# ScalarE takes the first norm's root of unit n + 1 ahead of its copy of the turned rows of unit n

## The chip, the cores and the metric

One Trainium2 chip, of which one core runs the kernel. The metric is the time of one execution on the device, in microseconds, as the median of several runs. The engines are TensorE (PE; its weight loads are PEld), VectorE (DVE), ScalarE (ACT), GpSimd (POOL) and SyncE (SP), which issues most of the transfers. Each engine runs its own program in order, and they meet by semaphores.

## The reference, cut to what matters

A block of a small vision model, on x of shape (2, 256, 32, 32) in fp32: a norm over the channels, an attention with 1x1 convolutions, and a mixture of eight experts on the tokens.

```python
def _ln_c(v, eps=1e-06):
    m = jnp.mean(v, axis=1, keepdims=True)
    s = jnp.var(v, axis=1, keepdims=True)
    return (v - m) / jnp.sqrt(s + eps)
...
# in _L0_conv_ref, with xf = _ln_c(x) as (b, c, n)
g_vec = jnp.mean(jax.nn.softmax(xf, axis=2) * xf, axis=2)
g_map = jnp.broadcast_to(g_vec[:, :, None], (b, c, n))
kv_in = jnp.concatenate([g_map, xf], axis=1)
q = _proj(_proj(xf, q_w1, q_g1, q_b1), q_w2, q_g2, q_b2)
k = _proj(_proj(kv_in, k_w1, k_g1, k_b1), k_w2, k_g2, k_b2)
v = _proj(kv_in, v_w, v_g, v_b)
sim = jnp.einsum('bcn,bcm->bnm', q, k) * tc ** (-0.5)
attn = jax.nn.softmax(sim, axis=-1)
ctx = jnp.einsum('bnm,bcm->bcn', attn, v)
out = _proj(ctx, o_w, o_g, o_b)
...
x = x + _L0_conv_ref(_ln_c(x), ...)
t = _to_tokens(x)
t = t + _L0_ffn_ref(_ln_t(t), ...)   # top 2 of 8 experts, 256 -> 1024 -> 256, gelu
x = _from_tokens(t, x)
```

The change lies in the first line of work, `_ln_c(x)`: the norm of each of the 2048 positions over its 256 channels.

## The kernel before, in words

The 2048 rows (positions) are cut into 4 units of 512, and a unit into 4 blocks of 128 rows. For each unit the first norm goes through five engines:

- SyncE loads the unit's rows into `x1` (L359), one transfer of 512 KB each, the four of them issued first, with the query weights between.
- VectorE, `row_stats(u)`: four `bn_stats` (L854) and four `bn_aggr` (L858) give mean and variance, `mv1`; each aggregate raises `var_ready`.
- ScalarE, `root(u)` (L598): one small activation takes the square root of the four variances into `rstd1`, and raises `std_ready`.
- VectorE, `row_norm(u)`: waits for that, takes the reciprocal in place (L864, raises `rstd_ready`), and norms blocks 0 and 1 of the unit into `xn2` (L867, `normed`). GpSimd waits for `rstd_ready` and norms blocks 2 and 3 (L450, `normed_more`).
- TensorE, `turn_rows(u)` (L1254): eight transposes of 128x128 against the identity, two a block, into two PSUM banks; the last raises `xn_turned`. Units 0 and 2 share banks, and so do units 1 and 3, so the transposes of unit u also wait for the copy of unit u - 2.
- ScalarE, `channels(u)` (L604): one copy of 128x1024 from PSUM into `x_cn`, the rows in channel order; it raises `xcn_ready`.

VectorE's program has, unit after unit, `row_stats(u)` and `row_norm(u)`, so the statistics of the next unit stand behind the norms of this one. TensorE's program is: transposes of units 0 and 1; first query projection of unit 0 (`project("q1", 0)`, L1271, needs `xcn_ready` of unit 0); transposes of unit 2; q1 of unit 1; second query projection q2 of unit 0 (L1266); transposes of unit 3; q2 of unit 1; then the query projections of units 2 and 3, then the key and value projections. ScalarE takes each projection out of PSUM (`take`, L622), and its program mixes these with the copies; behind the take of q2 of unit 1 come a table load and the exponentials of the softmax over positions for batch 0 (L636), which need the maximum that VectorE takes over units 0 and 1 (L872). Two more takes of q1 follow.

Behind all this stand the key and value projections, 16 steps of attention with the output convolution, the second norm and routing, and from about 170 us on the experts, which fill the rest of the time. The order on each engine is written out by hand; no scheduler decides it. TensorE begins the kernel with nine matmuls on ones (L1240).

Of the kernel before, what the change touches and what calls it, by code (L numbers as in the profile page):

```python
# [52 lines left out]
def metaformer_kernel(nc, x_tok_d, q1_d, q2_d, k1_d, k2_d, v_d, o_d, aff_d, og_d, ob_d,  # L53
                      wg_d, w1_d, b1_d, w2_d, b2_d, out_d):
    ctx = ExitStack()
    with ctx:
# [351 lines left out]
        def _(pool):  # L408
# [162 lines left out]
            for e in range(E):  # L571
                _, t1, odd, more = expert_bounds(pool, e)

                odd1 = pool.value_load(bounds[0:1, 1, e:e + 1], min_val=0, max_val=E)
                with pool.If(odd):
                    tile(t0, e, t0 * 2 + odd0, WIDE)
                with pool.Else():
                    tile(t0, e, t0 * 2 + odd0, 2)
                with pool.If(more):
                    with pool.Fori(t0 + 1, t1) as t:  # L580
                        tile(t, e, t * 2 + odd1, 2)
                t0 = t1
                odd0 = odd1
# [6 lines left out]
        def _(act):  # L590
# [5 lines left out]
            def root(u):  # L596
                act.wait_ge(var_ready, BLKU * (u + 1))
                act.activation(rstd1[:, u * BLKU:(u + 1) * BLKU], mv1[:, u * BLKU:(u + 1) * BLKU, 1], ACT.Sqrt,  # L598
                               bias=eps_c[:, :]).then_inc(std_ready, 1)

            def channels(u):

                act.wait_ge(xn_turned, u + 1)
                act.activation(x_cn[:, :, u * UNIT:(u + 1) * UNIT], banks[:, TURN_BANK[u]:TURN_BANK[u] + 2, :],  # L604
                               ACT.Copy).then_inc(xcn_ready, 1)
# [25 lines left out]
            def global_exp(b):  # L631
                act.wait_ge(gmax_ready, b + 1)
                for k in range(KC):
                    if b:
# [2 lines left out]
                                   ACT.Exp, bias=gmax[:, b, k:k + 1], accum_out=gsum[:, b, k:k + 1]  # L637
                                   ).then_inc(gexp_ready, 1)

            for u in range(2):  # L640
                root(u)
                channels(u)
            root(2)
            root(3)
            act.wait_ge(wq_loaded, 16 * 3)
            take("q1", 0)
# [9 lines left out]
            for b in range(B):  # L656
                u, w = 2 * b, 2 * b + 1
# [170 lines left out]
        def _(dve):  # L828
# [388 lines left out]
            for e in range(E):  # L1217
                _, t1, odd, more = experts[e]
                with dve.If(odd):
                    tile(t0, e, WIDE, True)  # L1220
                with dve.Else():
                    tile(t0, e, 2, True)
                with dve.If(more):
                    with dve.Fori(t0 + 1, t1) as t:
                        tile(t, e, 2, False)
                t0 = t1
# [379 lines left out]
```

## Time and profile before

| what | value |
|---|---|
| median of 3 runs | 427.2 us (425.88 to 430.45) |
| profiled execution | 429.23 us, of which the span of its core is 427.5 |
| mean granted TensorE clock | 0.918 of full speed |
| TensorE busy, matmuls | 372.4 us, 87% of the span |
| TensorE busy, weight loads | 333.8 us, 78% |
| VectorE busy | 264.9 us, 62% |
| ScalarE busy | 247.6 us, 58% |
| GpSimd busy | 177.3 us, 41% |
| chain that ended last | TensorE 38%, GpSimd 10%, issue 8% |

The span runs from the first to the last instruction; the rest of an execution's time lies around it. The granted clock is the share of TensorE's full speed that the chip allowed: 1.00 is 2.4 GHz and 0.50 is 1.2 GHz. In a timeline, a row is a run of like instructions, with its start, its length from the first one's start to the last one's end, their count, and in brackets how long the engine stood idle ahead of them and what released it. Rows of one engine can overlap by a tenth of a microsecond, since an instruction begins before the one ahead of it has drained.

### The profile page before, as it was taken

How to read it: one execution, taken by the hardware profiler on the slowest of the kernel's cores; microseconds unless marked ns; L12 is line 12 of the kernel's file. 1: busy time of each engine (PE TensorE's matmuls, PEld its weight loads, DVE VectorE, ACT ScalarE, POOL GpSimd, SP SyncE). 2: the span in 40 equal slices, each digit the busy share in tenths (PEclk: the TensorE clock that was granted, in tenths of full speed). 3: DMA queues.
4: the chain of work that ended last, by engine and by line, in shares of the span. 5: the costliest groups of instructions: out<-in, count | busy, mean ns of one | idle time of the engine just before them, and what ended most of it. 6: DMA issues, size and time to landing. Idle time of an engine off the chain costs nothing.

```text
span 427.5 us, 8138 instructions
## 1 busy us (share of the span) xinstructions
PE 372.4 (87%) x2476; PEld 333.8 (78%) x2477; DVE 264.9 (62%) x693; ACT 247.6 (58%) x522; POOL 177.3 (41%) x271
## 2 busy tenths in 40 slices
PE   5789969997998866999969999989999999989960
PEld 4435557886787856999969998989989999989960
DVE  5668487797889896364438444874448754834430
ACT  1386656656525872575539555795557955764530
POOL 5620000003045444326642665656546546656553
PEclk9699999999996555799998999999999999999995
DMA  8710000000010764609322832378323724232333
GB/s 277 231 37 2 0 1 2 0 2 1 2 61 39 299 204 133 236 15 255 57 53 27 246 62 54 49 237 244 60 56 46 240 40 71 39 53 53 49 52 35
DMA packets 22966, 38.63 MB, mean 90 GB/s; under 512 B 2576, under 2 KB 17296, under 8 KB 22800
## 3 DMA queue, kind: packets, MB, share of 16 engines
q0 software_dynamic: 8032, 12.82, 17.9%
q1 hardware_dynamic: 14896, 25.41, 17.2%
q8 instruction: 11, 0.18, 0.2%
q14 instruction: 27, 0.22, 0.2%
HBM read 28.85 MB, written 9.37 MB: 89 GB/s over the span
## 4 chain that ended last, share of the span: by engine, by line
PE 38%; POOL 10%; issue 8%; DVE 2%; POOLq 1%; DMA 1%; DVEq 1%; ACT 1%; ACTq 0%
POOL xg L521 8%; PE banks L1534 6%; PE banks L1233 6%; PE banks L1234 6%; PE banks L1235 6%; PE banks L1536 5%; PE banks L1538 5%; PE banks L1511 3%; DVE h_lo L1183 1%; DVE y_out L1207 1%; PE banks L1566 1%; POOL idx_in L516 1%; DMA xg<-xn_rows,idx_in 1%; POOL idx_out L559 1%; POOL out_rows L567 0%
## 5 line engine op out<-in xcount | busy, mean ns | idle before, releaser
L790 ACT ACTIVATE h_raw<-banks,b1t 128x256 f32<-128x256 f32 (+1 forms) x136 | 67.6, 497 | 86.7 <-PE banks L1235 86.1
L1183 DVE TENSOR_TENSOR h_lo<-h_raw,h_hi 128x256 fp32r<-128x256 f32 (+1 forms) x136 | 58.0, 441 | 65.0 <-ACT h_hi L793 63.0
L1534 PE MATMUL banks<-w_hi,h_hi 128*128 128x256 f32 x288 | 84.3, 293 | 9.2 <-DVE h_lo L1183 9.2
L1234 PE MATMUL banks<-x_lo,w_hi 128*128 128x256 f32 (+1 forms) x272 | 79.3, 292 | 3.5 <-issue 3.5
L1536 PE MATMUL banks<-w_lo,h_hi 128*128 128x256 f32 x288 | 81.4, 283 | 0.0
L1538 PE MATMUL banks<-w_hi,h_lo 128*128 128x256 f32 x288 | 81.4, 283 | 0.0
L1233 PE MATMUL banks<-x_hi,w_hi 128*128 128x256 f32 (+1 forms) x272 | 80.2, 295 | 0.8 <-issue 0.8
L1235 PE MATMUL banks<-x_hi,w_lo 128*128 128x256 f32 (+1 forms) x272 | 79.4, 292 | 0.0
L567 POOL DMA_INDIRECT out_rows<-y_out,idx_out x36 | 62.5, 1736 | 33.7 <-DVE y_out L1207 27.9
L521 POOL DMA_INDIRECT xg<-xn_rows,idx_in x57 | 57.1, 1001 | 27.9 <-POOL idx_in L516 16.3
L793 ACT ACTIVATE h_hi<-banks,b1t 128x256 fp32r<-128x256 f32 (+1 forms) x136 | 67.4, 495 | 0.0
L1534 PEld LDWEIGHTS banks<-w_hi,h_hi 128*128 128x128 f32 x288 | 55.2, 192 | 11.9 <-DVE h_lo L1183 11.8
L1235 PEld LDWEIGHTS banks<-x_hi,w_lo 128*128 128x128 f32 x272 | 52.7, 194 | 3.6 <-issue 3.6
L1536 PEld LDWEIGHTS banks<-w_lo,h_hi 128*128 128x128 f32 x288 | 55.2, 192 | 0.0
L1538 PEld LDWEIGHTS banks<-w_hi,h_lo 128*128 128x128 f32 x288 | 55.1, 191 | 0.0
L1233 PEld LDWEIGHTS banks<-x_hi,w_hi 128*128 128x128 f32 x272 | 52.8, 194 | 1.9 <-issue 1.8
L1234 PEld LDWEIGHTS banks<-x_lo,w_hi 128*128 128x128 f32 x272 | 52.8, 194 | 0.0
L472 POOL TENSOR_TENSOR rt<-rstd_i,rhv 128x4 f32<-128x4 f32 x12 | 2.5, 211 | 97.9 <-DVE rstd_i L990 97.2
L1190 DVE TENSOR_TENSOR w_lo<-w_raw,w_hi 128x512 fp32r<-128x512 f32 x56 | 38.5, 688 | 1.0
L803 ACT ACTIVATE w_hi<-w_raw 128x512 fp32r<-128x512 f32 x56 | 36.8, 656 | 0.0
L680 ACT ACTIVATE pt_hi<-banks 128x512 fp32r<-128x512 f32 x32 | 17.5, 596 | 20.9 <-PE banks L1348 20.9
L1207 DVE TENSOR_SCALAR y_out<-y_sum,score 128x256 f32<-128x256 f32 x36 | 11.0, 350 | 23.1 <-POOLq L562 22.8
(219 smaller groups left out, 681.0 us busy)
## 6 DMA issues: line engine op xcount, KB each, us to landing
w_raw<-in_w SPq DMA_DIRECT2D x16, 1024.0 KB, 8.2
xn_rows<-xn SPq DMA_DIRECT2D x2, 1056.0 KB, 5.0
x<-in_x_tok SPq DMA_DIRECT2D x4, 512.0 KB, 4.9
out_rows<-x SPq DMA_DIRECT2D x1, 2048.0 KB, 9.3
b2b<-in_b SPq DMA_DIRECT2D x1, 1024.0 KB, 4.8
xg<-xn_rows,idx_in POOLq DMA_INDIRECT x57
out_rows<-y_out,idx_out POOLq DMA_INDIRECT x36, 4.0
out_rows<-x POOLq DMA_DIRECT2D x1, 384.0 KB, 3.2
```

The source lines that it names most:

```text
L521: pool.indirect_dma_start(xg[:, i, :], None, xs_d, bass.IndirectOffsetOnAxis(ap=idx_in[:, i:i + 1], axis=0)).then_inc(x_gathered, 16)
L567: pool.indirect_dma_start(out_d, bass.IndirectOffsetOnAxis(ap=idx_out[:, i:i + 1], axis=0), y_out[:, i, :], None, compute_op=ALU.add).then ...
L790: act.activation(h_raw[j % RING][:, 0:w], banks[:, j % RING, 0:w], ACT.Gelu, bias=bias)
L793: act.activation(h_hi[:, j, 0:w], banks[:, j % RING, 0:w], ACT.Gelu, bias=bias).then_inc(gelu_done, 1)
L1183: dve.tensor_tensor(h_lo[:, j, 0:w], h_raw[j % RING][:, 0:w], h_hi[:, j, 0:w].bitcast(F32), ALU.subtract).then_inc(h_split, 1)
L1190: dve.tensor_tensor(w_lo[(e + 1) % 2][:, c], w_raw[(e + 1) % 2][:, c], w_hi[(e + 1) % 2][:, c].bitcast(F32), ALU.subtract).then_inc(w_spli ...
L1233: pe.matmul(out, a_hi, b_hi, start=start, stop=False)
L1234: pe.matmul(out, a_hi, b_lo, start=False, stop=False)
L1235: return pe.matmul(out, a_lo, b_hi, start=False, stop=stop)
L1534: pe.matmul(out, h_hi[:, j, r], w_hi[e % 2][:, c], start=j == 0 and i < 2, stop=False, skip_group_check=width == WIDE)
L1536: pe.matmul(out, h_hi[:, j, r], w_lo[e % 2][:, c], start=False, stop=False, skip_group_check=width == WIDE)
L1538: ins = pe.matmul(out, h_lo[:, j, r], w_hi[e % 2][:, c], start=False, stop=j == HJ - 1, skip_group_check=width == WIDE)
```

## The change

In ScalarE's program the roots of units 1 and 2 are taken one place earlier: that of unit n + 1 now stands ahead of the copy of unit n. The root of unit 3 keeps its place. No instruction is added or removed, and no other engine's program is touched.

```diff
--- before.py
+++ after.py
@@ -637,10 +637,10 @@
                                    ACT.Exp, bias=gmax[:, b, k:k + 1], accum_out=gsum[:, b, k:k + 1]
                                    ).then_inc(gexp_ready, 1)
 
+            root(0)
             for u in range(2):
-                root(u)
+                root(u + 1)
                 channels(u)
-            root(2)
             root(3)
             act.wait_ge(wq_loaded, 16 * 3)
             take("q1", 0)
```

ScalarE at the start of its program, before: the rows on `rstd` are the roots, the rows on `x_cn` the copies, the rows on `q1r` and `q2r` the takes, and the brackets name the semaphores waited for.

```order
L593 ACT_TABLE_LOAD
L593 ACTIVATE warm<-eps_c 128x1 [waits consts_made]
L598 ACTIVATE rstd<-mv,eps_c 128x4 [waits var_ready]
L604 ACTIVATE x_cn<-banks 128x2x512 [waits xn_turned]
L598 ACTIVATE rstd<-mv,eps_c 128x4 [waits var_ready]
L604 ACTIVATE x_cn<-banks 128x2x512 [waits xn_turned]
L598 ACTIVATE rstd<-mv,eps_c 128x4 [waits var_ready] x2
L622 ACTIVATE q1r<-banks,aff 128x512 [waits proj_ready,wq_loaded]
```

The roots of units 2 and 3 stood together behind the second copy. The same place of ScalarE's program with the change:

```order
L593 ACT_TABLE_LOAD
L593 ACTIVATE warm<-eps_c 128x1 [waits consts_made]
L598 ACTIVATE rstd<-mv,eps_c 128x4 [waits var_ready] x2
L604 ACTIVATE x_cn<-banks 128x2x512 [waits xn_turned]
L598 ACTIVATE rstd<-mv,eps_c 128x4 [waits var_ready]
L604 ACTIVATE x_cn<-banks 128x2x512 [waits xn_turned]
L598 ACTIVATE rstd<-mv,eps_c 128x4 [waits var_ready]
L622 ACTIVATE q1r<-banks,aff 128x512 [waits proj_ready,wq_loaded]
```

Now two roots stand ahead of the first copy and one ahead of the second; the table loads are where they were. The other end of the relay is TensorE, whose program is the same in both kernels; this is its piece from the first query projection of unit 0 over the transposes of unit 2 to the projection of unit 1.

```order
L1271 MATMUL banks<-x_cn,w_q 128x512 [waits xcn_ready,wq_loaded]
L1271 MATMUL banks<-x_cn,w_q 128x512
L1254 MATMUL banks<-ident,xn 128x128 [waits normed,xcn_ready]
L1254 MATMUL banks<-ident,xn 128x128
L1254 MATMUL banks<-ident,xn 128x128 [waits normed]
L1254 MATMUL banks<-ident,xn 128x128
L1254 MATMUL banks<-ident,xn 128x128 [waits normed_more]
```

Nothing moved here: the transposes of unit 2 stand behind the projection, and wait in turn for VectorE's norms, for the copy of unit 0 and for GpSimd's norms.

## Rows read from the trace of the kernel before

**Rows 1.** Timeline of ScalarE, 4 to 30 us: start us, us, engine, line, tiles.
```profile
10.57 1.02 ACT L604 ACTIVATE x_cn<-banks 128x1024 f32<-128x1024 f32 x1 [3.67 <-PE banks L1254]
11.49 0.29 ACT L598 ACTIVATE rstd<-mv,eps_c 128x4 f32<-128x4 f32 x1
15.43 1.02 ACT L604 ACTIVATE x_cn<-banks 128x1024 f32<-128x1024 f32 x1 [3.65 <-PE banks L1254]
16.35 0.29 ACT L598 ACTIVATE rstd<-mv,eps_c 128x4 f32<-128x4 f32 x1
19.41 0.30 ACT L598 ACTIVATE rstd<-mv,eps_c 128x4 f32<-128x4 f32 x1 [2.77 <-DVE mv L858]
19.61 0.76 ACT L622 ACTIVATE q1r<-banks,aff 128x512 f32<-128x512 f32 x1
...
23.50 1.02 ACT L604 ACTIVATE x_cn<-banks 128x1024 f32<-128x1024 f32 x1
...
25.21 1.28 ACT L636 ACT_TABLE_LOAD   x1
...
28.78 1.43 ACT L622 ACTIVATE q1r<-banks,aff 128x512 f32<-128x512 f32 x2
```

**Rows 2.** Timeline of VectorE, 4 to 22 us.
```profile
9.28 0.35 DVE L858 BATCH_NORM_AGGREGATE mv<-bst 128x2 f32<-128x6 f32 x4
11.81 0.18 DVE L864 RECIPROCAL rstd<-rstd 128x4 f32<-128x4 f32 x1 [2.18 <-ACT rstd L598]
...
12.85 1.39 DVE L854 BATCH_NORM_STATS2 bst<-x 128x6 f32<-128x256 f32 x4
14.16 0.35 DVE L858 BATCH_NORM_AGGREGATE mv<-bst 128x2 f32<-128x6 f32 x4
...
19.02 0.35 DVE L858 BATCH_NORM_AGGREGATE mv<-bst 128x2 f32<-128x6 f32 x4
```

**Rows 3.** Timeline of GpSimd, 4 to 30 us.
```profile
7.22 2.57 POOL L450 TENSOR_SCALAR xn<-x,mv,rstd 128x256 f32<-128x256 f32 x2 [3.39 <-DVE rstd L864]
12.09 2.56 POOL L450 TENSOR_SCALAR xn<-x,mv,rstd 128x256 f32<-128x256 f32 x2 [2.30 <-DVE rstd L864]
16.95 2.56 POOL L450 TENSOR_SCALAR xn<-x,mv,rstd 128x256 f32<-128x256 f32 x2 [2.30 <-DVE rstd L864]
```

**Rows 4.** Timeline of TensorE's matmuls, 4 to 25 us.
```profile
9.85 0.69 PE L1254 MATMUL banks<-ident,xn 128*128 128x128 f32 x2 [0.64 <-POOL xn L450]
12.50 1.70 PE L1254 MATMUL banks<-ident,xn 128*128 128x128 f32 x6 [1.96 <-DVE xn L867]
14.71 0.69 PE L1254 MATMUL banks<-ident,xn 128*128 128x128 f32 x2 [0.51 <-POOL xn L450]
15.19 3.62 PE L1271 MATMUL banks<-x_cn,w_q 128*128 128x512 f32 x4
18.60 1.41 PE L1254 MATMUL banks<-ident,xn 128*128 128x128 f32 x8
19.85 1.88 PE L1271 MATMUL banks<-x_cn,w_q 128*128 128x512 f32 x4
...
22.42 1.04 PE L1254 MATMUL banks<-ident,xn 128*128 128x128 f32 x8
```

**Rows 5.** The line that issues the four loads of x, and their landing.
```profile
L359 SPq DMA_DIRECT2D x<-in_x_tok x4: 382/426/467, 0.8 to 2.7; - x4
...
DMA to landing us min/median/max: 3.4/4.9/6.3
```

**Rows 6.** Windows of TensorE: stretch, its length, busy us (count), granted clock, DMA.
```profile
8.90:19.10 10.20, 7.08 (x19) 0.50 0.98 295
19.00:19.20 0.20, 0.20 (x4) 0.88 0.07 26
128.50:131.60 3.10, 3.10 (x16) 0.50 0.22 90
171.80:175.90 4.10, 4.10 (x20) 0.50 0.94 356
```

## The prediction

> **What bounds the kernel now.** I read the page first, and in it the busy shares: TensorE is busy 87% of the span, VectorE and ScalarE about 60%. The page's chain of the work that ended last is shown from 167 us on only, so the front is read from the timelines of the four engines, each for its own waits, and then from the windows, for the granted clock. The edit touches nothing behind ScalarE's copy for unit 1, so the first 30 us are what has to be understood.
>
> The front is a relay by units of 512 rows. VectorE makes the statistics, ScalarE the root, VectorE the reciprocal and two norms, GpSimd the other two norms, TensorE turns the four blocks, ScalarE copies the result to channel order. [rows 1] show ScalarE's place in it. It finishes the copy for unit 0 at 11.59 and only then takes the root of unit 1, at 11.49 by the overlapped records. That root's input was ready long before: VectorE's last aggregate for unit 1 starts at 9.28 and ends at 9.63 [rows 2]. The engine stood idle for 3.67 us before the copy, waiting for TensorE. VectorE then waits 2.18 us for the root. The same happens for unit 2: the statistics end at 14.51 [rows 2], the copy for unit 1 runs at 15.43, the root at 16.35. VectorE can't run ahead, since its program is in order and the reciprocal stands ahead of the next unit's statistics.
>
> GpSimd is the slowest hand: its two norms of a unit take 2.56 us [rows 3], and TensorE's last two transposes of unit 1 start at 14.71, just behind GpSimd's end at 14.65. TensorE does the first projection next, 15.19 to 18.60, then unit 2's transposes, and from there it waits little: two projections, unit 3's transposes, and so on, each row beginning as the one before it ends [rows 4]. ScalarE's copy of unit 3 (23.50) follows the transposes that end at 23.46, its next take follows at once, and the table load for the exponentials comes at 25.21. Behind it the exponentials and the two takes at 28.78 run back to back, while TensorE stands still. So **from unit 1's transposes to 28.78 there is one path: TensorE up to 23.5, ScalarE from there**, and what shortens the front moves all that follows.
>
> **The change, part by part.** Nothing is added or removed: still four roots of 0.29 us and four copies of 1.02 us. Three roots move. No table load appears between them, as the printed order shows.
>
> *Root of unit 1.* It is ready when the aggregates end, 9.63. In unit 3, where ScalarE stands waiting at the root, it starts 0.04 after them (19.37 to 19.41, [rows 1, 2]). So it starts at 9.67 in place of 11.49: **1.82 us earlier**. The reciprocal comes 0.32 behind the root (11.49 to 11.81) at 9.99; GpSimd 0.28 behind that, at 10.27, in place of 12.09. GpSimd is free since 9.79 (its unit 0) and TensorE since 10.54, so neither takes anything back. Unit 1's transposes end 1.82 earlier, at 13.58, and the copy for unit 1 starts at 13.61, not 15.43. The copy for unit 0 keeps its 10.57, since the root ahead of it ends at 9.97.
>
> *Root of unit 2.* VectorE's statistics start at 12.85 - 1.82 = 11.03 and end 1.66 later (12.85 to 14.51), at 12.69. Unit 2's rows must be there by 11.03 and unit 3's by 14.1: the last of the four loads is issued at 2.7 and the longest takes 6.3 us to land, so 9.0 at the latest [rows 5]. The root takes 12.73 to 13.02, in place of 16.35: 3.62 earlier. What queues behind it on ScalarE is the copy for unit 1, wanted at 13.58: **0.56 us of cover**. GpSimd does unit 2 at 13.33 to 15.89, not 16.95 to 19.51.
>
> *Root of unit 3.* Its order against the copy for unit 1 is as before. Statistics start at 14.08, end at 15.75 (the same 1.66); the root at 15.79 meets a free ScalarE. GpSimd ends unit 3 at 16.39 + 2.56 = 18.95, and its reader on TensorE comes behind 20, so the rest of this gain is worth nothing. VectorE's maximum for batch 0 comes earlier too; its reader, the exponential, stands behind ScalarE's takes and gains nothing by that.
>
> *TensorE.* The first projection starts at 15.19 - 1.82 = 13.37 and occupies 3.41 us (15.19 to 18.60), to 16.78. Now unit 2's norms have been ready since 15.89, so its transposes wait for nothing. At the full clock eight occupy 0.88 us (22.42 to 23.30). At the low clock two occupy 0.48 (14.71 to 15.19), or 0.44 taken as twice the fast time; I take 1.76 for eight. In the trace the granted clock is at its lower level, 1.2 GHz, from 8.9 on and returns to 2.4 GHz at 19.05 (its mean of 0.88 over 19.0 to 19.2 leaves 0.05 us at 0.50, [rows 6]), 3.86 after the projection began. If it comes back as long after the same work, at 17.23, then 0.45 of the slow 1.76 is spent, and the other 74% take 0.66: the transposes end at 16.78 + 0.45 + 0.66 = 17.89. Before it was 19.85: **1.96 us earlier**, of which 0.14 is a wait for GpSimd that is gone.
>
> ScalarE's take of the first projection then starts at about 17.0; it was held until 19.61 by the root of unit 3, but its reader on TensorE comes one projection at the full clock later (half of 3.41), at 17.89 + 1.71 = 19.60, and finds it done. All behind keeps its lengths: 1.96 earlier at 23.5, at 25.21 and at 28.78. The key and value weights were issued by about 9 and the projections that want them stand behind 28 us, so no load holds them.
>
> **The sum.** 1.96 us off an execution of 429.23 (span 427.5, 1.7 around it) is 427.3. The median of the runs shown is 427.2, 2.0 below the profiled one, so I subtract from the median: 425.2.
>
> **A rule against the row.** The row: the clock is low from 8.9 to 19.05, and returns inside a stretch in which TensorE has been busy without a gap since 14.71 [rows 4, 6]. My sum lets it return by the work. The Trainium skill, page "TensorE: Matmul & The Clock Gate", section "What's actually happening", says the chip's looking at activity is free-running and isn't reset by the kernel's start, so the switch falls differently from run to run. By this rule the sum may keep 19.05 as the moment, or take an earlier one. One trace can't tell which; it gives rivals 1 and 2 their chances.
>
> **The rivals.**
> 1. *The clock returns at the same moment of the trace, 19.05.* Transposes all slow: 16.78 + 1.76 = 18.54. The next projection is slow for 0.51 and loses half of it, 0.25. Gain 19.85 - 18.54 - 0.25 = 1.06. Time 426.1. For it: nothing that moves the clock's own times is in the edit. Against: busy work starts earlier too. Chance 0.17.
> 2. *The clock returns sooner*, since TensorE's pause between units 0 and 1 (10.54 to 12.50) is gone. The bound is GpSimd's end of unit 2 at 15.89: last pair of transposes 15.95 to 16.17, gain 19.85 - 16.17 = 3.68. Half way between this and 1.96 is 2.8. Time 424.4, at the far end 423.5. For it: denser work from 10.68 on. Against: in the trace the clock stayed low through the transposes of unit 1 too. Chance 0.20.
> 3. *The other side: the later low stretches grow.* All that follows 28.78 runs 2 us earlier, and the clock need not follow. One spell of low clock lasted 3.1 us with TensorE always busy; the end of the long one, 171.8 to 175.9, is 4.1 us of pure TensorE at half speed [rows 6]. Each lengthened by such a spell costs half of it, 1.6 to 2.0. The place is the first transposes and products of the expert stage. Beyond 4 us more of low clock under pure TensorE the gain is eaten; slower by 1% needs (4.3 + 2.0) x 2 = 12.6 us. I take 8 us: time 429.2. For it: the runs of before differ by 4.6 us with no edit at all. Against: the spells can as well get shorter. Chance 0.08.
> 4. *It doesn't do what it says.* If unit 2's rows landed after 11.6 (11.03 and the 0.56 of cover), the root ahead would hold the copy of unit 1, and past 13.4 it would be later than before: 427.2 and up. [rows 5] put the landing 2.6 us short of the first point. Chance 0.05.
>
> **How the numbers follow.** The forecast has 0.50: 425.2. A measurement of this kernel tells about 1% from no change, 4.3 us, so faster means under 422.9 and slower over 431.5. The runs of before lie from 425.88 to 430.45, 1.3 below and 3.3 above their median; a median is surer, and I give it 1.5 to either side. Under 422.9 lie a third of rival 2 (0.07), whose far end is 0.6 above it, and a tenth of the forecast (0.05): 0.12. Over 431.5 lies half of rival 3, 0.04. The rest is 0.84. The range reaches from rival 2's far end less some of the spread to short of rival 3's time: 421.9 to 428.5.
>
> **What would show it.** In the new timeline the root of unit 1 at 9.67, ahead of the copy at 10.57; GpSimd's norms at 10.3, 13.3 and 16.4; no idle of VectorE over 0.4 us ahead of a reciprocal; the copy for unit 1 at 13.6; unit 2's transposes beginning at 16.8 and ending near 17.9; the table load at 23.2; the two takes behind the exponentials at 26.8. The windows give the clock's return near 17.2 (forecast), 19.0 (rival 1) or before 16 (rival 2). The prediction fails if the table load moves by less than 1 us or more than 3, or if it moves by 2 and the span doesn't: then the gain is lost to the clock or to a wait behind 30 us.

## The result and the profile after

The changed kernel takes 424.96 us as the median of 10 executions (424.21 to 427.16). The kernel before, run beside it and now over 10 executions, takes 428.35 (425.88 to 430.45). The ratio is 0.9925, with a 95% interval of 0.9904 to 0.9947: 3.2 us faster, by between 2.3 and 4.1. (The ratio is not the quotient of the two medians, which differ by 3.4.) The forecast was 425.2 and "within 1%", and both hold. But the median it was taken from, 427.2 over three executions, was 1.2 us below what ten gave, and the forecast step of 1.96 us lies below the interval of the measured one.

| | before | after |
|---|---|---|
| profiled execution | 429.23 us | 427.16 us |
| its span | 427.5 us | 425.4 us |
| TensorE busy, matmuls | 372.4 us | 372.0 us |
| ScalarE busy | 247.6 us | 248.1 us |
| VectorE busy | 264.9 us | 264.9 us |
| GpSimd busy | 177.3 us | 177.6 us |

The work is the same to half a microsecond; what went is waiting. ScalarE in the changed kernel, timeline from 4 us on (start, length, engine, line, tiles, in brackets the idle time ahead and who ended it), which answers to [rows 1]:

```profile
9.68 0.30 ACT L598 ACTIVATE rstd<-mv,eps_c 128x4 f32<-128x4 f32 x1 [2.77 <-DVE mv L858]
10.59 1.02 ACT L604 ACTIVATE x_cn<-banks 128x1024 f32<-128x1024 f32 x1 [0.61 <-PE banks L1254]
12.75 0.30 ACT L598 ACTIVATE rstd<-mv,eps_c 128x4 f32<-128x4 f32 x1 [1.14 <-DVE mv L858]
13.63 1.02 ACT L604 ACTIVATE x_cn<-banks 128x1024 f32<-128x1024 f32 x1 [0.59 <-PE banks L1254]
15.82 0.30 ACT L598 ACTIVATE rstd<-mv,eps_c 128x4 f32<-128x4 f32 x1 [1.16 <-DVE mv L858]
...
23.07 1.28 ACT L636 ACT_TABLE_LOAD   x1
...
26.65 1.43 ACT L622 ACTIVATE q1r<-banks,aff 128x512 f32<-128x512 f32 x2
```

The root of unit 1 stands at 9.68 and not at 11.49, that of unit 2 at 12.75 and not at 16.35. Both roots now start when VectorE's aggregates are done (`DVE mv`), within 0.04 us, and the copies behind them still wait for TensorE, 0.61 and 0.59 us. The second of these is the cover that was worked out as 0.56: the time by which the root ends before the copy's input is there. The table load at 23.07 was at 25.21, and the two takes at 26.65 were at 28.78: 2.14 and 2.13 us. Two reciprocals of VectorE, after, against the one at 11.81 in [rows 2] that had waited 2.18 us:

```profile
10.01 0.18 DVE L864 RECIPROCAL rstd<-rstd 128x4 f32<-128x4 f32 x1 [0.36 <-ACT rstd L598]
...
13.08 0.18 DVE L864 RECIPROCAL rstd<-rstd 128x4 f32<-128x4 f32 x1 [0.36 <-ACT rstd L598]
```

GpSimd's norms of units 1 to 3, which answer to [rows 3] (units 1 and 2 at 12.09 and 16.95 there):

```profile
10.29 2.56 POOL L450 TENSOR_SCALAR xn<-x,mv,rstd 128x256 f32<-128x256 f32 x2 [0.48 <-DVE rstd L864]
13.36 2.56 POOL L450 TENSOR_SCALAR xn<-x,mv,rstd 128x256 f32<-128x256 f32 x2 [0.50 <-DVE rstd L864]
16.42 2.56 POOL L450 TENSOR_SCALAR xn<-x,mv,rstd 128x256 f32<-128x256 f32 x2 [0.50 <-DVE rstd L864]
```

TensorE's matmuls from the last transposes of unit 1 on, against [rows 4]:

```profile
12.91 0.69 PE L1254 MATMUL banks<-ident,xn 128*128 128x128 f32 x2 [0.52 <-POOL xn L450]
13.39 3.61 PE L1271 MATMUL banks<-x_cn,w_q 128*128 128x512 f32 x4
16.80 1.07 PE L1254 MATMUL banks<-ident,xn 128*128 128x128 f32 x8
17.71 1.88 PE L1271 MATMUL banks<-x_cn,w_q 128*128 128x512 f32 x4
19.43 1.02 PE L1266 MATMUL banks<-q1r,w_q 128*128 128x512 f32 x2
```

Turning unit 1 ends at 13.60, the first projection runs 13.39 to 16.80, and the transposes of unit 2, which had waited in part for GpSimd, take 0.91 us (16.80 to 17.71) and not 1.25. The next projection starts at 17.71 in place of 19.85. This is the whole of the gain in this pair of executions: 2.14 us at the second projection (the one of unit 1), 2.14 at the table load, 2.1 in the span.

One row misleads. The window of TensorE over the first projection (stretch, its length, busy us, granted clock, DMA) says:

```profile
13.40:16.60 3.20, 3.20 (x5) 1.00 0.98 351
```

A clock of 1.00, and yet four matmuls of 512 columns occupy 3.41 us, exactly as in the trace of before, where [rows 6] give 0.50. Four such matmuls at the full clock occupy 1.72 (17.71 to 19.43 in the timeline above). So this projection ran at 1.2 GHz although its window says 2.4. The windows of this trace show nothing below 1.00 ahead of 126 us. The trace of before has the same blind start: its opening matmuls take 421 ns or more each and the shortest transposes of unit 0 take 272 ns, all under a window of 1.00, and the first low clock in its windows is the fall at 8.8. In the changed kernel's trace the transposes of unit 0 take 421 ns or more, so its clock was low already. The eight transposes at 16.80 take 0.91 us, close to the 0.88 of the full clock, so the clock came back at about 16.8; this is read from lengths, not from the record.

### The profile page after: what moved, and what is told of

Its sections match the earlier page's. It is cut to its first block, busy times and chain, and to the rows that moved or that the text cites. A ratio compares the mean times of both kernels' runs of the same rounds, so it can differ in the third digit from the quotient of the medians.

```text
span 425.4 us, 8138 instructions
## 1 busy us (share of the span) xinstructions
PE 372.0 (87%) x2476; PEld 333.7 (78%) x2477; DVE 264.9 (62%) x693; ACT 248.1 (58%) x522; POOL 177.6 (42%) x271
## 4 chain that ended last, share of the span: by engine, by line
PE 38%; POOL 10%; issue 8%; DVE 2%; DMA 1%; POOLq 1%; DVEq 1%; ACT 1%; ACTq 0%
POOL xg L521 8%; PE banks L1534 6%; PE banks L1233 6%; PE banks L1234 6%; PE banks L1235 6%; PE banks L1536 5%; PE banks L1538 5%; PE banks L1511 3%; DVE h_lo L1183 1%; DVE y_out L1207 1%; PE banks L1566 1%; DMA xg<-xn_rows,idx_in 1%; POOL idx_in L516 1%; POOL idx_out L559 1%; POOL out_rows L567 0%
## 5 line engine op out<-in xcount | busy, mean ns | idle before, releaser
L680 ACT ACTIVATE pt_hi<-banks 128x512 fp32r<-128x512 f32 x32 | 17.5, 596 | 20.9 <-PE banks L1348 20.9
```

## The experiments

Twelve runs followed. The theory: there is one path through the front (all work ahead of the table load), each unit's blocks come late by what ScalarE's root is late, the front gives between 1 and 3.7 us as the clock returns late or early, and all behind it keeps its length. The rivals: both moves carry the gain alike; the clock and not the order is what costs; a second gain lies behind the front. The table gives each kernel's time against the kernel before in the same comparison (ratio, its interval, and the ratio's distance from 1 in us). Its last column says where the table load stands in the profiled execution, which measures the front alone.

| kernel | ratio (95%) | us against before | table load |
|---|---|---|---|
| before, second profile | 0.9993 (0.9969 to 1.0016) | -0.3 | 25.23 |
| changed, first | 0.9925 (0.9904 to 0.9947) | -3.2 | 23.07 |
| changed, second | 0.9924 (0.9894 to 0.9953) | -3.2 | 22.39 |
| changed, third | 0.9919 (0.9888 to 0.9951) | -3.5 | 23.35 |
| root of unit 1 alone | 0.9971 (0.9949 to 0.9993) | -1.2 | 23.39 |
| root of unit 2 alone | 1.0006 (0.9986 to 1.0025) | +0.3 | 25.62 |
| all roots first | 1.0072 (1.0042 to 1.0102) | +3.1 | 28.11 |
| before, extra matmuls | 0.9946 (0.9918 to 0.9975) | -2.3 | 24.74 |
| changed, extra matmuls | 0.9897 (0.9856 to 0.9938) | -4.4 | 21.61 |
| changed, 1 memset late | 0.9962 (0.9937 to 0.9988) | -1.6 | 23.92 |
| changed, 2 memsets late | 0.9953 (0.9927 to 0.9979) | -2.0 | 24.84 |
| changed, three norms on VectorE | 0.9935 (0.9910 to 0.9960) | -2.8 | 21.61 |
| the same, extra matmuls | 0.9912 (0.9882 to 0.9943) | -3.8 | 21.62 |

**The changed kernel again, twice.** No edit.

> The changed kernel once more, beside the runs of the two parts. Theory (one path through the front, shortened at unit 1): the table load for the exponentials stands near 23.1 us in place of 25.2, and the time is 2.1 us under the kernel before. Rival (there is a second gain somewhere behind 30 us): the time is 3 us or more under it while the table load moves by only 2.1.

> The changed kernel a third time. Theory (the front gives 2.1 to 2.8 us by the moment of the clock's return, the rest is the same on average): the table load between 22.3 and 23.6, and a ratio that, with the two measured so far, tends to 2.1 to 2.8 us under the kernel before. Rival (a second gain of about 1 us behind the front): again 3.2 us or more.

The step holds: -3.2 and -3.5 us, not the 2.1 to 2.8 that the theory expected. The rival of both, a second gain behind the front, was marked by 3 us or more and by 3.2 or more, and both times met it; the first mark also asked for a table load that moves by 2.1 alone, and there it moved by 2.8. The front isn't a constant, though. TensorE in the second profile of the changed kernel:

```profile
13.38 2.93 PE L1271 MATMUL banks<-x_cn,w_q 128*128 128x512 f32 x4
16.15 1.04 PE L1254 MATMUL banks<-ident,xn 128*128 128x128 f32 x8
17.02 1.88 PE L1271 MATMUL banks<-x_cn,w_q 128*128 128x512 f32 x4
```

Two windows of TensorE in the same trace, with the granted clock as the number behind the count:

```profile
15.30:15.50 0.20, 0.20 (x1) 0.53 0.91 348
15.50:15.70 0.20, 0.20 (x1) 1.00 1.01 410
```

The clock came back at 15.5, inside the first projection, which then occupied 2.77 us and not 3.41; the transposes began at 16.15, held by nothing, since GpSimd ends unit 2 at 15.9. The table load stands at 22.39, 2.82 us ahead of before: rival 2 of the prediction, with its own number. The third profile has its transposes from 16.80 to 17.99 and the table load at 23.35, 1.86 ahead; from their 1.19 us, against 0.88 fast and 1.76 slow, the clock came back at about 17.4. So the front gives 1.9 to 2.8 us, 2.3 as the mean of three.

**The kernel before again.** No edit.

> The kernel before against itself, as a measure of what the comparison can tell, and one more profile of it. Theory: the table load at 24.9 to 25.7 us, whatever the moment at which the clock comes back in the front, since GpSimd's norms of unit 2 end at 19.5; what differs between two executions lies behind 30 us, in where the stretches of low clock fall, and the span from the table load to the end is anything from 400 to 402.5. The ratio within 0.3% of 1. Rival (the front decides the spread of the runs): the table load differs by over 1 us from 25.2.

The front and the ratio are as expected. The rest is not: from the table load to the end this profile takes 405.2 us, where 400 to 402.5 was expected and the first profile has 402.3. TensorE in this second profile of before:

```profile
15.21 2.89 PE L1271 MATMUL banks<-x_cn,w_q 128*128 128x512 f32 x4
17.94 0.89 PE L1254 MATMUL banks<-ident,xn 128*128 128x128 f32 x6
19.59 0.44 PE L1254 MATMUL banks<-ident,xn 128*128 128x128 f32 x2 [0.77 <-POOL xn L450]
19.87 1.88 PE L1271 MATMUL banks<-x_cn,w_q 128*128 128x512 f32 x4
```

Here, too, the clock returned early: the projection occupies 2.73 us, not 3.41, and the transposes begin at 17.94 in place of 18.60. It buys nothing: the last two wait 0.77 us for GpSimd, the second projection starts at 19.87 and the table load stands at 25.23, within 0.02 of the first profile. In the kernel before, an early clock is lost at GpSimd; in the changed one it is kept. That is why the change is worth more than 1.96 at the table load in an execution with an early clock.

**The two halves of the change.**

```diff
 root of unit 1 alone
 root(0)
-channels(0)
 root(1)
+channels(0)
 channels(1)
 root(2)
 root(3)
```

```diff
 root of unit 2 alone
 root(0)
 channels(0)
 root(1)
-channels(1)
 root(2)
+channels(1)
 root(3)
```

> Only the root of unit 1 goes ahead of the copy of unit 0; the root of unit 2 stays behind the copy of unit 1. Theory: unit 1's transposes end 1.8 us earlier, unit 2's norms on GpSimd end at 17.7 instead of 15.9, which delays the transposes of unit 2 by 0.1 us at most if the clock is low until about 17, so the table load stands at 23.2 and the time is within 0.5 us of the whole change. Where the clock comes back sooner, GpSimd's 17.7 binds and up to 1.5 us of the gain are missing. Rival (both moves carry the gain alike): the table load at 24 or later, the time 1 us above the whole change.

> Only the root of unit 2 goes ahead of the copy of unit 1; the root of unit 1 stays behind the copy of unit 0. Theory: unit 1's transposes stay at 15.4, the first projection at 15.2, and the only gain is that GpSimd ends unit 2 at 17.7 and not at 19.5; unit 2's transposes begin at 18.6 as before and end at most 0.2 us earlier with the clock as in the kernel before, up to 1.2 with an earlier clock. Time 0 to 1 us under the kernel before. Rival (both moves carry it): 1 to 1.6 us.

The profile of each half follows. The root of unit 1 alone, TensorE:

```profile
13.38 3.42 PE L1272 MATMUL banks<-x_cn,w_q 128*128 128x512 f32 x4
16.63 0.82 PE L1255 MATMUL banks<-ident,xn 128*128 128x128 f32 x6
17.76 0.44 PE L1255 MATMUL banks<-ident,xn 128*128 128x128 f32 x2 [0.31 <-POOL xn L450]
18.03 1.88 PE L1272 MATMUL banks<-x_cn,w_q 128*128 128x512 f32 x4
```

The projection starts at 13.38, as in the full change. The last transposes of unit 2 then wait 0.31 us for GpSimd (worked out: ready at 17.7, here 17.76) and the second projection starts at 18.03. With the root of unit 2 moved as well that bound is at 15.9. So in the front the first move carries 1.8 us, and the second adds what an early clock allows: 0.0 to 1.0 in the three profiles of the full change, 0.5 on average. The time doesn't agree. Root of unit 1 alone takes 1.2 us off (0.3 to 2.2), where within 0.5 of the whole change was expected, and beside it in the same comparison the whole change took 3.2 off, a median of 424.24 against 426.02. So the rival's mark in the time, 1 us above the whole change, is met, and its mark at the table load, 24 or later, is not (23.39). Of those 2 us the front accounts for 0.5; the rest isn't explained.

The root of unit 2 alone, TensorE:

```profile
15.20 3.62 PE L1272 MATMUL banks<-x_cn,w_q 128*128 128x512 f32 x4
18.61 1.81 PE L1255 MATMUL banks<-ident,xn 128*128 128x128 f32 x8
20.26 1.88 PE L1272 MATMUL banks<-x_cn,w_q 128*128 128x512 f32 x4
```

And GpSimd's norms of units 1 and 2 in the same trace:

```profile
12.10 2.56 POOL L450 TENSOR_SCALAR xn<-x,mv,rstd 128x256 f32<-128x256 f32 x2 [2.30 <-DVE rstd L865]
15.17 2.56 POOL L450 TENSOR_SCALAR xn<-x,mv,rstd 128x256 f32<-128x256 f32 x2 [0.51 <-DVE rstd L865]
```

GpSimd has unit 2 ready 1.8 us earlier (15.17 and not 16.95), TensorE doesn't use it, as its first projection still starts at 15.20. In this execution the clock was late and the transposes took 1.65 us; the time is that of the kernel before within its interval (0.6 us less to 1.1 more). That the second move alone is worth its rival's 1 to 1.6 us is out, and in the front the two don't carry the gain alike. The two times, -1.2 and +0.3, do not add up to the -3.2 of both. Some of that is as the theory has it, since the second move pays only behind the first; the size is not.

**All roots first.**

```diff
 root(0)
 root(1)
-channels(0)
 root(2)
-channels(1)
 root(3)
+channels(0)
+channels(1)
```

> All four roots stand ahead of the first copy. Theory: the root of unit 3 is ready at 15.75, so the copy of unit 0 starts at 16.1 and not at 10.6, the first projection at about 17.2 and not at 13.4 (it waits for that copy); the table load stands at 27 to 28 us, and the time is 1.5 to 3 us above the kernel before. Rival (an earlier root is always better since the copy has cover): no later than the changed kernel.

+3.1 us, the table load at 28.11, each a tenth beyond what was expected. ScalarE's root of unit 3, its two copies and the table load:

```profile
15.81 0.30 ACT L598 ACTIVATE rstd<-mv,eps_c 128x4 f32<-128x4 f32 x1 [2.77 <-DVE mv L859]
16.01 1.92 ACT L604 ACTIVATE x_cn<-banks 128x1024 f32<-128x1024 f32 x2
...
28.11 1.28 ACT L636 ACT_TABLE_LOAD   x1
```

TensorE's first projection in the same trace:

```profile
17.16 3.75 PE L1272 MATMUL banks<-x_cn,w_q 128*128 128x512 f32 x4 [3.57 <-ACT x_cn L604]
```

The copy of unit 0 went from 10.59 to 16.01, since the root of unit 3 waits for its statistics until 15.8. The projection waits 3.57 us for it, and starts at 17.16, as worked out. An earlier root is no good in itself: it may stand ahead of a copy as long as it ends before the copy's input comes.

**Extra matmuls, to have the clock back early.** They go into a bank that is written anew before anything is read from it, and compute nothing that is used.

```diff
-            for _ in range(9):
+            for _ in range(15):
                 pe.matmul(banks[:, 7, 0:P], ones[:, :], ones[:, :], start=True, stop=True)
...
                 for j in range(BLKU):
+                    if u < 2:
+                        for _ in range((1, 1, 1, 2)[j] if u == 0 else (4, 1, 1, 2)[j]):
+                            pe.matmul(banks[:, 3, 0:P], ones[:, :], ones[:, :], start=True, stop=True)
```

> The kernel before with extra matmuls on ones: 15 in place of 9 at the start, and a few in TensorE's waits among the transposes of units 0 and 1, into a bank that nobody reads. They compute nothing that is used. Theory: the clock is back before the first projection (15.2), which then takes 1.7 us; but the transposes of unit 2 wait for GpSimd, whose norms of unit 2 end at 19.5, so they end at 19.8 as before and the table load stays at 25.2. Time within 0.5 us of the kernel before. Rival (the low clock in the front is what costs): 1.5 us or more under it.

> The changed kernel with the same extra matmuls. Theory: GpSimd's norms of unit 2 end at 15.9, the first projection at full clock ends at 15.1, so the transposes of unit 2 end at 16.2 and the table load stands at 21.5 us: 3.7 us ahead of the kernel before, and 0.9 to 1.6 us ahead of the changed kernel's profiles (22.4 and 23.1). Time 3.5 to 4.5 us under the kernel before. Rival (GpSimd or ScalarE binds earlier than worked out): the table load at 22.4 or later, and no difference from the changed kernel.

In the kernel before with them, ScalarE:

```profile
10.34 1.02 ACT L604 ACTIVATE x_cn<-banks 128x1024 f32<-128x1024 f32 x1 [3.43 <-PE banks L1257]
11.26 0.29 ACT L598 ACTIVATE rstd<-mv,eps_c 128x4 f32<-128x4 f32 x1
...
24.74 1.28 ACT L636 ACT_TABLE_LOAD   x1
```

TensorE in the same trace:

```profile
14.76 1.88 PE L1274 MATMUL banks<-x_cn,w_q 128*128 128x512 f32 x4
16.98 1.36 PE L1257 MATMUL banks<-ident,xn 128*128 128x128 f32 x6 [0.34 <-DVE xn L867]
19.10 0.44 PE L1257 MATMUL banks<-ident,xn 128*128 128x128 f32 x2 [0.77 <-POOL xn L450]
```

The projection runs at the full clock, 14.76 on, the transposes begin at 16.98, and the last two stand 0.77 us until GpSimd is done: the clock alone is lost there, as the theory has it. What I had missed is the 0.47 us ahead of that. At the full clock the transposes of unit 0 end sooner, the copy starts at 10.34 and not 10.57, and the root behind it at 11.26 and not 11.49; twice 0.23 makes the table load's 24.74. The time fell by 2.3 us, by at least 1.1, where I expected under 0.5; the rival, that the low clock in the front is what costs, was marked by 1.5 or more. The front accounts for 0.5 of it; the rest isn't explained, so by the time this rival is not out. In the changed kernel with them, TensorE:

```profile
13.18 1.88 PE L1274 MATMUL banks<-x_cn,w_q 128*128 128x512 f32 x4
14.90 0.82 PE L1257 MATMUL banks<-ident,xn 128*128 128x128 f32 x6
15.98 0.44 PE L1257 MATMUL banks<-ident,xn 128*128 128x128 f32 x2 [0.26 <-POOL xn L450]
16.25 1.88 PE L1274 MATMUL banks<-x_cn,w_q 128*128 128x512 f32 x4
```

The second projection starts at 16.25 (worked out: 16.2) and the table load stands at 21.61, 3.6 us ahead of before. Both are met, and so is the time, 4.4 us under before, the lowest of all kernels here, though its interval (2.7 to 6.2) overlaps that of the change.

**The relay late by a known amount.** One or two idle memsets of 128x1024 on VectorE ahead of the first statistics, on the changed kernel.

```diff
+            for i in range(2):      # or range(1)
+                dve.memset(prob[i][:, :], 0.0)
             for u in range(UNITS):
                 row_stats(u)
```

> The changed kernel with one idle memset of 128x1024 on VectorE ahead of the first statistics, about 1.1 us, which shifts the whole relay and nothing else. Theory (one path, and all behind it keeps its length): the time is 1.1 us above the changed kernel, 2.1 under the kernel before. Rival (the measured gain of 3.2 holds a part that comes from how the rest of the kernel lies against the chip's clock, and not from the front): the time moves by something else than 1.1, such as 0 or 2.

> The same with two memsets, about 2.1 us. Theory: 2.1 us above the changed kernel, 1.1 under the kernel before. Rival: the front shift that the profiled pair shows (2.1) is given back whole, and the time is that of the kernel before, or it differs from the step of late1 by much more or less than 1.1.

The memsets delay the root of unit 1 by 1.0 and 2.1 us (10.69 and 11.76 against 9.68). Measured are -1.6 and -2.0 us against before. From the change's -3.3 (mean of three) that is 1.7 and 1.3 later, where the table loads moved by 1.0 and 1.9 from the mean of 22.9. The first is met within its uncertainty of about 1.1 us. The second is 0.8 short of its mark of 2.1, and one memset and two can't be told apart by time: the step between them, expected as 1.1 more, is 0.4 less. With two memsets the kernel still takes at least 0.9 us less than before, with a table load only 0.4 ahead. The memsets suggest that a late front costs time; a slope of 1 they don't show.

**Three of four norms on VectorE**, with and without the extra matmuls.

```diff
-        DVE_NORMS = 2
+        DVE_NORMS = 3
```

> The changed kernel with three of a unit's four norms on VectorE and one on GpSimd. Theory (after the change a unit's blocks are late by GpSimd's two norms of 2.56 us): unit 1's last norm is ready at about 12.0 and not 12.85, the first projection starts at about 12.5 and not 13.4, and the table load comes 0.9 us earlier than in the changed kernel, at 21.5 to 22.2; the time 0.9 us under the changed kernel. Rival (VectorE, whose turn per unit grows from 3.07 to 3.48 us, is late instead): no gain or a loss.

> The same with the extra matmuls on ones. Theory: the clock is back before the first projection at 12.4, which ends at 14.1; unit 2's last norm is ready at about 15.5, so its transposes end at 15.8, and the table load stands at 21.1 us, 0.5 ahead of the kernel with the extra matmuls and two norms each, 4.1 ahead of the kernel before. Time 4 to 5 us under the kernel before. Rival: VectorE's longer turn makes unit 2 and 3 late and the table load stays at 21.6.

TensorE without the extra matmuls:

```profile
12.84 2.58 PE L1271 MATMUL banks<-x_cn,w_q 128*128 128x512 f32 x4
15.26 1.04 PE L1254 MATMUL banks<-ident,xn 128*128 128x128 f32 x8
```

ScalarE in the same trace:

```profile
16.79 0.30 ACT L598 ACTIVATE rstd<-mv,eps_c 128x4 f32<-128x4 f32 x1 [2.18 <-DVE mv L858]
17.00 0.76 ACT L622 ACTIVATE q1r<-banks,aff 128x512 f32<-128x512 f32 x1
...
20.79 0.80 ACT L622 ACTIVATE q2r<-banks,aff 128x512 f32<-128x512 f32 x1
21.61 1.28 ACT L636 ACT_TABLE_LOAD   x1
```

The first projection starts 0.55 us earlier than in the changed kernel, at 12.84 and not at 12.5 as worked out: unit 1's norms are ready at 12.0, but its eight transposes begin at 11.03 and occupy 1.81 us in a row at the low clock, so TensorE itself is last. GpSimd, 1.40 us a unit, binds no more. But the table load stands at 21.61 and 21.62 without and with the extra matmuls, the same as with two norms and the extra matmuls (21.61). From the root of unit 3 at 16.79 to the table load ScalarE has no idle time at all: take, copy, take, take, copy, take. What starts this row is VectorE: that root waits 2.18 us for the statistics (`DVE mv`), since VectorE's turn per unit is 3.39 us here (root to root, 13.40 to 16.79) and not 3.07. So the rival of the second run, a table load that stays at 21.6 by VectorE's longer turn, is what came, with ScalarE's row behind it. The first projection ends at 15.26, and its take stands behind this root until 17.00: a small case of what all roots first shows; no run here tries this take ahead of the root. The times, -2.8 and -3.8 us, are not below the change's beyond the intervals; the first was expected at 0.9 under the change, and is 0.5 above it.

**Where the rest of the difference is.** Cut at the table load, at the start of the last exponential of the attention, at the first and the last transpose of the expert stage, the traces give in us:

| kernel | to table load | attention | routing | experts | end |
|---|---|---|---|---|---|
| before | 25.2 | 88.2 | 56.9 | 239.7 | 17.5 |
| before, second | 25.2 | 89.6 | 57.5 | 240.6 | 17.5 |
| changed | 23.1 | 88.2 | 57.4 | 239.2 | 17.5 |
| changed, second | 22.4 | 89.1 | 57.0 | 236.6 | 17.5 |
| changed, third | 23.4 | 88.2 | 57.1 | 238.1 | 17.6 |
| root of unit 1 alone | 23.4 | 89.1 | 57.0 | 236.8 | 17.5 |
| root of unit 2 alone | 25.6 | 89.6 | 57.0 | 236.3 | 17.5 |
| all roots first | 28.1 | 89.6 | 56.8 | 237.8 | 17.6 |
| before, extra matmuls | 24.7 | 89.6 | 57.0 | 237.9 | 17.5 |
| changed, extra matmuls | 21.6 | 88.2 | 57.0 | 234.9 | 17.5 |
| 1 memset late | 23.9 | 88.2 | 57.2 | 237.0 | 17.5 |
| 2 memsets late | 24.8 | 88.2 | 57.2 | 236.8 | 17.5 |
| three norms | 21.6 | 89.1 | 57.4 | 237.9 | 17.6 |
| three norms, extra | 21.6 | 89.1 | 57.4 | 234.1 | 17.6 |

No column behind the first follows the edits one for one. The expert stage runs the same program in all and takes anything from 234.1 to 240.6 us; two profiles of one and the same kernel differ by up to 2.6 us there. That is large beside the 3 to 6 us over which the executions of one kernel spread. The two profiles of before are the longest of all there (239.7 and 240.6), and the two with the change and the extra matmuls are the shortest (234.9 and 234.1). The traces hold one thing that goes with it: a long stretch of low clock that begins between 130 and 140 us lasts 41.0 us in eight of the fourteen and 34.1 in six, and the expert stage takes 238.2 us on average in the eight and 236.4 in the six. Both profiles of before have the long form, and so have two of the change's three. Whether the front decides the form, or chance does, so few profiles can't tell.

The attention takes three values, 88.2, 89.1 and 89.6, and they go with a short stretch of low clock: none between 25 and 120 us, one at about 56, or one about 5 us behind the table load. The last kind costs 1.4 us and appears in four of the five executions whose table load stands at 24.7 or later with no memset, and in none of the other nine. It would be a second gain of the change, of up to 1 us on average, if it were the rule. Fourteen single profiles are too few to say so, and nothing here tells why an earlier front should escape it.

Taken together, each kernel's time against before and its table load against the 25.2 of before agree within the interval of the time in eight of ten kernels, the change (as the mean of its three, 2.3 and 3.3) only at the interval's edge. The two outside are the kernel before with the extra matmuls (front 0.5, time 2.3) and the two memsets (0.4 and 2.0). The order of the front is shown to set the table load; that the table load sets the time one for one is only roughly so.

## Why the prediction was right

**The bound.** Held for the front. The path was TensorE to 23.5 and ScalarE from there, and every shift of the second projection arrived whole at the table load: 2.14 and 2.14 in the first profile, 2.83 and 2.82 in the second, 1.86 and 1.86 in the third. One reading beside it was wrong: TensorE doesn't stand still behind the table load. In the trace of before it projects from 24.16 to 27.76 and then waits 1.93 us for the take at 28.78, so it is idle for the last part alone. Nothing in the sum hangs on that.

**Root of unit 1**, forecast 9.67, measured 9.68; GpSimd 10.27 against 10.29; the copy of unit 1 13.61 against 13.63. **Root of unit 2**, 12.73 against 12.75, with a cover of 0.56 against the 0.59 that the copy still waited. **Root of unit 3**, 15.79 against 15.82. No load was late, and rival 4 falls: in no profile of the changed kernel did a root hold a copy.

**The clock** was the one term with two ends, and both the middle and one end turned up. The forecast let it return at 17.23 and had the second projection start at 17.89; the three profiles have it back at about 16.8, 15.5 and about 17.4, and the projection at 17.71, 17.02 and 17.99. Gains at the table load of 2.14, 2.82 and 1.86 stand against 1.96 (forecast), 2.8 (rival 2) and 1.06 (rival 1). Rival 1's moment, 19.05, came in none. Rival 2 deserved more than its 0.20, since I had read one trace of before, and in it a late return and an early one would have looked the same from ScalarE: the second profile shows that GpSimd's norms hide the difference. The Trainium skill, page "TensorE: Matmul & The Clock Gate", section "What's actually happening", says that the switch falls differently from run to run. The traces agree: 15.5 in one execution of the changed kernel, 16.8 or later in the two others. Why it does, no run here shows.

**The size.** The front gives 2.3 us by the mean of three profiles, the measurement says 3.2, 3.2 and 3.5 with lower ends of 2.3, 2.0 and 2.1. In the front the term that was too small is the clock's, by 0.3. About 1 us is left over, and the prediction had put the change behind the front at nothing. The lower ends of the three comparisons just reach the front's 2.3, but all three came out above, so it may be real; it would then sit behind the front, where one profile of each kernel can't weigh it against swings of 2 to 3 us. That stays open, and so do the 1.8 us of the kernel before with extra matmuls, the 1.6 with two memsets, and the 1.5 that the root of unit 1 alone lacks against the whole change.

**The base.** That the absolute number hit within 0.3 us is luck: the base was 1.2 us too low and the step 1.3 too small, and the two errors cancel. By the ratio, 0.9954 was forecast and 0.9925 measured, which is 424.0 from the base of 427.2: inside the range of 421.9 to 428.5, but nearer to rival 2's 424.4 than to the forecast's 425.2.

**Rival 3**, longer stretches of low clock later on, did not show: in the first pair the three stretches between 100 and 400 us lie 2.2 us earlier with the work and are as long as before (47.8 us together in both). The spell that the prediction read as 3.1 us was cut short by its window; it lasts 3.4.

## What to carry to other kernels

On an engine with a program in order, a short instruction that others wait for belongs ahead of a long one whose own input is late, as long as it is done before the long one's input arrives; compare the arrival times in the trace, not the lengths. The same edit made once more (the root of unit 3 ahead of the first copy as well) turned 3 us of gain into 3 us of loss, since its input came 5 us behind the copy's. And where a stage is held by two things, here the clock and GpSimd, removing either alone showed little at the table load (0.5 us for the clock, nothing for GpSimd): read what would bind next, and give the range down to it. A shift that is plain in one trace is not yet the same shift in the time: moving one root gave 1.8 us at the table load and 1.2 in the time, moving both 2.3 and 3.3.

## What the runs showed of the hardware

- A trace can show a granted clock of 1.00 from its start over matmuls that ran at half of that: 0.85 us for each 512-column matmul of the first projection, against 0.43 at the full clock. In six of the eleven traces without extra matmuls the first projection is slower than at the full clock while no window of the first 25 us shows a low clock; in the other five the first low clock in the windows is a fall from 1.00. Read the clock of a kernel's first microseconds from the length of like instructions.
- The moment at which the clock returned in the front differed by over a microsecond between executions of one program, and the path by 1.0 us (table load at 22.39 to 23.35).
- The expert stage, the same instructions on the same data, took 234.1 to 240.6 us in 14 profiles. A change of 2 us at the front is plain in one profile, by the position of an instruction; in the total time it took six to twelve executions, and the intervals were still 0.8 to 1.8 us to either side.
